# RWKV-6 layer with a ternary feed-forward on one Trainium2 core: work moved between VectorE and GpSimd, weight setup inside tile 0, another layout of the last feed-forward

## The chip, the cores and the metric

One core of a Trainium2 chip runs the whole kernel. TensorE multiplies matrices and writes to PSUM. VectorE and ScalarE read and write PSUM and SBUF. GpSimd works on SBUF alone. SyncE issues the DMAs. The engines run side by side and wait for each other on semaphores. The metric is the device time of one launch in microseconds; smaller is better.

## What is computed

Input x is [4, 2048, 512] in float32. The reference computes, in float32:

```
x = layernorm(x + attention(x))          # RWKV-6 time mixing, 16 heads of 32
x = layernorm(x + feed_forward(x))

attention:  xx = x_prev - x
            mix = tanh((x + xx * maa_x) @ maa_w1) @ maa_w2        # five mixes: w k v r g
            r, k, v, g = projections of x + xx * (maa_* + mix)
            decay = exp(-exp(time_decay + tanh(xw @ td_w1) @ td_w2))
            y_t = r_t (S + u k_t v_t);  S = decay_t S + k_t v_t   # scan over 2048 steps
            out = (groupnorm(y) * ln_g + ln_b) * silu(g) @ Wo
feed_forward: h = gelu(x @ ternary(W_fc)); h = layernorm(h) * ln_w + ln_b; h @ ternary(W_proj)
ternary(W) = sign(W) * min(round(|W| / (mean|W| + eps)), 1)
```

## The kernel before

The sequence is cut into 32 tiles of 64 steps (4 sequences, 256 columns a tile). `tile` on each engine does the attention of tile `it`; the pieces of the feed-forward of tile `it - 1` stand between its steps (`ffn.up`, `ffn.down`, ...), so that engines that wait for one have the other. `over_tiles` writes out tiles 0 (without a feed-forward) and 1, loops over 2 to 31 and ends with `feed_forward(31).alone()`. All orders are written by hand; every engine does its instructions strictly in that order.

Steps that the change and the prediction speak of, in the order of a tile:
- The five mixes. TensorE multiplies the low-rank mix (L385), VectorE makes `(mix + maa) * XX` (L1100), GpSimd adds x (L916; VectorE for the decay input, L1111). `XX` is x_prev - x of the tile; VectorE made it in `differences` (L1082) near the end of the tile before. `mixed_by_x` (L1088) makes x + xx * maa_x from XX and XT, and TensorE multiplies it by W1 (L364, L367).
- XT, the next tile's x, is loaded by SyncE (L306) once GpSimd's fourth L916 is done.
- The chunk's scores are built in levels of 1, 2, 4, 8, 16. VectorE writes the even rows of RB (L1192) and ScalarE the odd ones; TensorE multiplies (L464, L481 for each level); between levels VectorE scales R and K (`scale_right` L1166, `scale_left` L1177), copies queries (L1156) and gathers the products into A (L1206, L1226).
- A is copied by strips into AB; GpSimd copies the last strip (L940). TensorE forms the output of each pair of sequences from the state (L522) and from AB (L538).
- VectorE copies the output (L1239), weighs it with ln_g and the gate (L1266), adds to the state (L1247), multiplies G by ln_b (L1277), and scales by the group deviation (L1279 to L1293). TensorE multiplies by Wo (L616).
- Feed-forward: `up` is on TensorE (L641) the hidden layer, on ScalarE GELU (L852), the scaled fp16 high part HHI (L861) and the square (L863), on VectorE the low part HLO (L1351) and the running sums (L1340, L1343). `down` (L660) multiplies by W_proj. `moments`, `product`, `normed`, `stored` finish a pair; GpSimd takes their inverse roots (L909, `finish`, `normed`) and adds the bias (L971).

Setup: VectorE sums |W| of eight pieces (L1021), quantises them (L1054, L1057), centres Wv (L1068 to L1074); TensorE multiplies the scaled ln_w and ln_b by W_proj (`against_second`), from which WSUM and BSUM are kept; GpSimd zeroes buffers (L877, L879) and splits the mix weights into high and low parts (L888, L890).

## Time and profile before

| | us |
|---|---|
| median of 3 runs | 3076.63 |
| lowest and highest | 3074.3, 3081.04 |
| the profiled execution, as timed | 3077.73 |
| its span in the trace | 3075.9 |
| TensorE busy | 2895.1 (94%) |
| VectorE busy | 2488.6 (81%) |
| ScalarE busy | 1928.0 (63%) |
| GpSimd busy | 931.3 (30%) |

A busy share is a mean over the whole launch. What ends a stretch is read from the waits and from the timelines: a row there has the start in us, the duration, engine, line, operation, output and inputs with shapes, how many were merged, and in brackets how long the engine had been idle and what ended it. "issue" means that the profile names no releaser.

### The profile page before, as it was taken

The numbers are of one execution on the slowest core, as the hardware profiler recorded it, in microseconds if no ns is written. First come the engines' busy times: TensorE is split into PE (matmuls) and PEld (weight loads), VectorE is DVE, ScalarE is ACT, GpSimd is POOL, SyncE is SP. The second block draws the span as 40 slices with busy tenths as digits, with TensorE's granted clock in tenths as the row PEclk, the third lists the DMA queues.
The fourth block names the chain that finished last, engine by engine and source line by source line (L and its number), as shares of the span: only waits on it lengthen the run. The fifth ranks groups of instructions, "written<-read, shape, count | busy, mean of one in ns | idle before, by whom it ended". The sixth has DMA issues, their size and how long they took to land.

```text
span 3075.9 us, 101635 instructions
## 1 busy us (share of the span) xinstructions
PE 2895.1 (94%) x40249; PEld 2120.9 (69%) x40249; DVE 2488.6 (81%) x5435; ACT 1928.0 (63%) x4079; POOL 931.3 (30%) x790
## 2 busy tenths in 40 slices
PE   1889999999999999999999999999999999999997
PEld 0666677777677777677777676777677777767775
DVE  8467887788887788888788898788798788888777
ACT  0456676666676666676666576666567666667664
POOL 1223232333322333332233322233323233332232
PEclk9899999999999999999999999999999999999999
DMA  5000000000000000000000000000000000000000
GB/s 215 8 15 23 13 19 23 22 16 22 13 23 19 23 16 23 16 20 19 23 16 22 16 19 19 23 15 22 23 13 19 23 22 16 23 13 23 19 23 15
DMA packets 22822, 73.40 MB, mean 24 GB/s; under 512 B 3104, under 2 KB 3360, under 8 KB 20768
## 3 DMA queue, kind: packets, MB, share of 16 engines
q1 hardware_dynamic: 22432, 67.10, 6.4%
q8 instruction: 379, 6.21, 0.8%
q14 instruction: 11, 0.09, 0.0%
HBM read 50.31 MB, written 16.78 MB: 22 GB/s over the span
## 4 chain that ended last, share of the span: by engine, by line
PE 63%; DVE 23%; issue 9%; ACT 3%; DVEq 1%; DMA 1%; SPq 0%; ACTq 0%; POOLq 0%; POOL 0%
PE psP L404 18%; PE psF L641 11%; PE psP L442 7%; PE psP L616 6%; PE psF L660 4%; DVE HLO L1351 4%; DVE ARENA L1226 2%; PE psY L522 2%; PE psY L538 2%; DVE SUMS L1343 2%; DVE ARENA L1100 2%; DVE ARENA L1088 2%; DVE ARENA L1166 2%; DVE ARENA L1290 1%; PE psP L424 1%
## 5 line engine op out<-in xcount | busy, mean ns | idle before, releaser
L404 PE MATMUL psP<-ARENA,WALL 128*128 128x256 f32 x3072 | 694.2, 381 | 2.7 <-ACT ARENA L733 2.7
L690 ACT ACTIVATE ARENA<-ARENA 32x512 f32<-32x512 f32 (+3 forms) x930 | 524.2, 564 | 188.1 <-DVE ARENA L1166 92.5
L404 PEld LDWEIGHTS psP<-ARENA,WALL 128*128 128x128 f32 x3072 | 574.9, 190 | 79.3 <-issue 1.8
L1351 DVE SCALAR_TENSOR_TENSOR HLO<-GG,FWB,HHI 128x128 f16<-128x128 f32 x1024 | 347.5, 400 | 283.4 <-ACT HHI L861 278.4
L641 PE MATMUL psF<-XHI,WFC 128*128 128x128 f16 x4096 | 488.2, 220 | 2.2 <-DVE ST L1367 1.9
L641 PE MATMUL psF<-XLO,WFC 128*128 128x128 f16 x4096 | 486.6, 220 | 0.0
L902 POOL TENSOR_TENSOR MT<-ARENA 32x256 fp32r<-32x256 f32 x330 | 319.3, 968 | 445.3 <-ACT ARENA L690 416.7
L916 POOL TENSOR_TENSOR ARENA<-ARENA,XT 128x1024 f32<-128x1024 f32 x128 | 278.6, 2177 | 506.3 <-DVE ARENA L1100 506.3
L641 PEld LDWEIGHTS psF<-XHI,WFC 128*128 128x128 f16 x4096 | 397.9, 98 | 41.0 <-issue 32.9
L641 PEld LDWEIGHTS psF<-XLO,WFC 128*128 128x128 f16 x4096 | 402.0, 98 | 17.6 <-issue 10.3
L660 PE MATMUL psF<-WPJ,HHI 128*128 128x512 f16 x1024 | 390.6, 381 | 13.5 <-ACT GG L852 13.5
L660 PE MATMUL psF<-WPJ,HLO 128*128 128x512 f16 x1024 | 388.8, 380 | 0.0
L909 POOL TENSOR_TENSOR FV<-FV,CF 128x1 f32<-128x1 f32 x64 | 67.8, 1059 | 1009.3 <-DVE FV L1373 1009.3
L861 ACT ACTIVATE HHI<-GG,FWB 128x128 f16<-128x128 f32 x1024 | 327.4, 390 | 25.5
L852 ACT ACTIVATE GG<-psF 128x512 f32<-128x512 f32 x256 | 152.2, 595 | 250.1 <-PE psP L404 135.9
L616 PE MATMUL psP<-WALL,ARENA 128*128 128x512 f32 x512 | 235.2, 602 | 4.3 <-DVE ARENA L1293 2.4
L442 PE MATMUL psP<-WALL,ARENA 128*128 128x512 f32 x512 | 224.9, 592 | 0.0
L690 ACT ACTIVATE ARENA<-psP 128x256 f32<-128x256 f32 (+1 forms) x192 | 93.8, 528 | 171.3 <-PE psP L404 171.3
L660 PEld LDWEIGHTS psF<-WPJ,HHI 128*128 128x128 f16 x1024 | 99.9, 98 | 128.7 <-issue 19.0
L852 ACT ACT_TABLE_LOAD x62 | 79.5, 1283 | 158.1 <-PE psP L442 153.1
L1100 DVE SCALAR_TENSOR_TENSOR ARENA<-psX,PAR,XX 128x256 f32<-128x256 f32 x324 | 141.0, 477 | 39.4 <-PE psX L385 39.4
L481 PEld LDWEIGHTS psW<-ARENA 128*32 128x32 f32 x8192 | 123.2, 111 | 68.9 <-issue 68.9
(165 smaller groups left out, 5160.4 us busy)
## 6 DMA issues: line engine op xcount, KB each, us to landing
XT<-x_ch SPq DMA_DIRECT2D x33, 520.0 KB, 3.4
ARENA<-x_tok SPq DMA_DIRECT2D x32, 512.0 KB, 4.7
out<-OUT SPq DMA_DIRECT2D x64, 256.0 KB, 2.1
WALL<-w_all SPq DMA_DIRECT2D x5, 1024.0 KB, 15.5
ARENA<-wfc SPq DMA_DIRECT2D x4, 1024.0 KB, 8.2
ARENA<-wpj SPq DMA_DIRECT2D x3, 1024.0 KB, 14.8
GG<-wpj SPq DMA_DIRECT2D x1, 1024.0 KB, 18.9
OUT<-w2a SPq DMA_DIRECT2D x8, 64.0 KB, 14.0
```

The source lines that it names most:

```text
L404: mm = pe.matmul(psP[:, P.bank(f"{name}{g}"), COLS * c:COLS * (c + 1)], WALL[:, w, k, 128 * (2 * g + c):128 * (2 * g + c + 1)], cc(XF[slot ...
L442: mm = pe.matmul(psP[:, P.bank(f"v{p}"), :], cc(XF[1], k)[:, 128 * p:128 * (p + 1)], WALL[:, W_V, k, :], start=(k == 0), stop=(k == KC - 1))
L616: mm = pe.matmul(psP[:, P.bank(f"wo{p}"), :], cc(YSB, k)[:, 128 * p:128 * (p + 1)], WALL[:, W_O, k, :], start=(k == 0), stop=(k == KC - 1))
L641: mm = pe.matmul(psF[:, F.bank(name), 128 * m:128 * (m + 1)], WFC[:, k, 128 * (4 * g + m):128 * (4 * g + m + 1)], x[:, p, k, :], start=(k ...
L660: mm = pe.matmul(psF[:, F.bank(f"pj_{p}"), :], h[:, m, :], WPJ[:, m, :], start=(m == 0 and h is HHI), stop=(m == MH - 1 and h is HLO))
L690: return act.activation(o, i, ACT.Copy)
L852: act.activation(GG[:, u % 2, 0, :], psF[:, F.bank(f"fc{g}_{p}"), :], ACT.Gelu).then_inc(f_act, 1)
L861: e = act.activation(HHI[:, k, :], GG[:, u % 2, 0, 128 * m:128 * (m + 1)], ACT.Copy, scale=FWB[:, 0, k:k + 1])
L902: pool.tensor_tensor(MT[f][rows(1 + 2 * (n % 2)), :], whole, high, ALU.subtract).then_inc(mt_low, 1)
L916: pool.tensor_tensor(v, v, xcur, ALU.add).then_inc(xf_ready, 1)
L1100: e = dve.scalar_tensor_tensor(out=cc(XF[(f + 1) % 2], k), in0=M_BANKS[M.bank(f"{name}{g}")][:, COLS * c:COLS * (c + 1)], scalar=PAR[:, k, ...
L1351: e = dve.scalar_tensor_tensor(out=HLO[:, k, :], in0=GG[:, u % 2, 0, 128 * m:128 * (m + 1)], scalar=FWB[:, 0, k:k + 1], in1=HHI[:, k, :], ...
```

## The change

It has four parts.
1. The mix weights (now one broadcast load a rank, on the semaphore `mixing_in`) and XT are loaded ahead of the other weights, and W_proj last. The constants' small steps come first on VectorE. Only W_fc is quantised ahead of tile 0. W_proj is summed, quantised and multiplied (`against_second`, in quarters) between the steps of tile 0, and WSUM and BSUM are kept at its end.
2. GpSimd computes XX (`differences`) after the bias, and multiplies G by ln_b in one operation; VectorE does neither any more.
3. GpSimd copies its AB strip ahead of the root of `finish`; VectorE does `up(1, 0)` ahead of `normed`.
4. The last feed-forward (`alone`) writes the hidden layer of pair 1 to four banks of the attention, between the `down` products of pair 0, and the product and sums of pair 1 to two others.

```diff
-        RAW = ([ARENA1[:, 2048 * k:2048 * (k + 1)] for k in range(4)] + [ARENA2[:, 2048 * k:2048 * (k + 1)] for k in range(3)]
-               + [GG[:, :, :, :].rearrange("p i s n -> p (i s n)")])
+        RAW = ([ARENA1[:, 6144:8192]] + [ARENA2[:, 2048 * k:2048 * (k + 1)] for k in range(3)]
+               + [ARENA1[:, 2048 * k:2048 * (k + 1)] for k in range(3)] + [GG[:, :, :, :].rearrange("p i s n -> p (i s n)")])
...
+            sp.dma_start(XT[:, :, :], x_ch[0]).then_inc(xt_in, 16)
+            sp.dma_start(W1[:, :, :], w1).then_inc(mixing_in, 16)
+            for f in range(5):
+                rank = w2a[rows(f), :] if f < 4 else w2b
+                sp.dma_start(W2RAW[f // 2][:, f % 2, :], rank.unsqueeze(0).broadcast_to([4, MIXR, C])).then_inc(mixing_in, 16)
+            sp.dma_start(WALL[:, W_V, :, :], w_all[:, W_V, :, :]).then_inc(values_in, 16)
+            for dst, src in ((TD1[:, :, :], td1), (TD2[0:DECR, :], td2), (TD2[DECR:2 * DECR, :], td2),
+                             (WALL[:, W_K, :, :], w_all[:, W_K, :, :])):
+                sp.dma_start(dst, src).then_inc(weights_in, 16)
+            for w in (W_R, W_G, W_O):
+                sp.dma_start(WALL[:, w, :, :], w_all[:, w, :, :]).then_inc(weights_in, 16)
...
+            def against_second(v, part):
+
+                if part == 0:
+                    pe.wait_ge(su_dve, 3)
+                    pe.wait_ge(quantised, 8)
+                for m in range(MH // 4 * part, MH // 4 * (part + 1)):
+                    for n, h in enumerate((VHI, VLO)):
+                        mm = pe.matmul(psF[:, v, :], h[:, v, m:m + 1].broadcast_to([128, 128]), WPJ[:, m, :],
+                                       start=(m == 0 and n == 0), stop=(m == MH - 1 and n == 1))
+                if part == 3:
+                    mm.then_inc(su_pe, 1)
+
+            pe.wait_ge(mixing_in, 16 * NMIXING)
...
+                if first:
+                    second_magnitude()
                 mix(it - 1, 3, "mr", wait_free)
+                if first:
+                    pe.wait_ge(su_dve, 5)
...
+                    if first:
+                        against_second(0, i)
...
-                    for p in range(PAIRS):
-                        for g in range(4):
-                            up(p, g)
-                        for part in range(4):
-                            down(j, p, part)
-                        stats(j, p)
+                    for g in range(4):
+                        up(0, g)
+                    pe.wait_ge(p_dve, P.read(tiles - 1, "wo1"))
+                    pe.wait_ge(w_dve, W.read(j, "xt1"))
+                    for g in range(4):
+                        hidden(LAST_UP[g], 1, g).then_inc(last_up, 1)
+                        down(j, 0, g)
+                    stats(j, 0)
+                    pe.wait_ge(m_dve, M.read(tiles, "mk1"))
+                    for g in range(4):
+                        pe.wait_ge(hlo_ready, 8 * j + 4 + g + 1)
+                        mm = projected(LAST_PRODUCT[:, :], g)
+                    mm.then_inc(last_product, 1)
+                    pe.wait_ge(sums_folded, 2 * (PAIRS * j + 1) + 2)
+                    summed(LAST_STATS).then_inc(last_stats, 1)
...
-            pool.wait_ge(quantised, 4)
-            pool.memset(ARENA1[:, 0:6144], 0.0).then_inc(su_pool, 1)
-            pool.wait_ge(quantised, 8)
-            pool.memset(ARENA2[:, 0:512], 0.0).then_inc(su_pool, 1)
...
+            def differences(it):
+                pool.wait_ge(xt_in, 16 * (it + 1))
+                pool.tensor_tensor(XX[:, :, :], xprev, xcur, ALU.subtract).then_inc(xx_ready, 1)
...
+                if first:
+                    pool.wait_ge(quantised, 7)
+                    pool.memset(ARENA1[:, 0:6144], 0.0).then_inc(su_pool, 1)
                 if ffn:
                     ffn.bias()
-                    ffn.finish()
+                differences(it + 1)
...
+                if ffn:
+                    ffn.finish()
...
+                pool.wait_ge(y_weighed, it + 1)
+                pool.tensor_tensor(G.rearrange("p (c t) -> p c t", c=KC), G.rearrange("p (c t) -> p c t", c=KC),
+                                   PAR[:, :, LN_B:LN_B + 1].broadcast_to([128, KC, COLS]), ALU.mult).then_inc(y_affine, 1)
 
                 pool.wait_ge(s_decayed, it + 1)
+                pool.wait_ge(y_affine, it + 1)
...
+            magnitudes(0, range(4), 6)
+            thresholds(0, psP[:, 0, 0:1], 6)
+            for k in range(4):
+                quantise(k, 8 + k)
+            dve.wait_ge(quantised, 4)
...
+            centred_values()
+            magnitudes(1, (0, 1), None)
...
+                if first:
+                    magnitudes(1, (2, 3), 16)
...
+                if first:
+                    thresholds(1, psF[:, 0, 0:1], 16)
+                    quantise(4, 18)
+                    quantise(5, 19)
...
+                if first:
+                    quantise(6, 20)
+                    quantise(7, 21)
...
-                dve.wait_ge(m_dve, M.read(it, "mg1"))
-                differences(it + 1)
...
                 if ffn:
+                    ffn.up(1, 0)
                     ffn.normed()
-                if ffn:
-                    ffn.up(1, 0)
...
-                dve.wait_ge(y_weighed, it + 1)
-                for k in range(KC):
-                    dve.tensor_scalar(cc(G, k), cc(G, k), PAR[:, k, LN_B:LN_B + 1], None, ALU.mult).then_inc(y_affine, 1)
...
+                    for g in range(4):
+                        up(0, g)
+                    fold(j, 0)
+                    for g in range(4):
+                        up(1, g)
+                    moments(j, 0)
+                    fold(j, 1)
+                    product(j, 0)
+                    normed(j, 0)
+                    stored(j, 0)
+                    moments(j, 1, last=True)
+                    product(j, 1, last=True)
+                    normed(j, 1)
+                    stored(j, 1)
```

GpSimd's order in a tile with a feed-forward (tile 1, which is written out; the loop's body has the same order). OUT is the bias step, CF the AB strip, FV and OSD the two roots, TOT the state's decay, MT the mix's low parts. Before:

```order
L916 TENSOR_TENSOR ARENA<-ARENA,XT 128x1024
L971 TENSOR_TENSOR OUT<-X,BSUM 128x512 x2
L909 TENSOR_TENSOR FV<-FV,CF 128x1
L940 TENSOR_TENSOR ARENA<-ARENA,CF 32x16x32
L948 TENSOR_TENSOR ARENA<-ARENA,TOT 128x512
L909 TENSOR_TENSOR OSD<-OSD,CF 128x1
L902 TENSOR_TENSOR MT<-ARENA 32x256 x10
```

And now:

```order
L964 TENSOR_TENSOR ARENA<-ARENA,XT 128x1024
L1029 TENSOR_TENSOR OUT<-X,BSUM 128x512 x2
L957 TENSOR_TENSOR XX<-XT 128x1024
L992 TENSOR_TENSOR ARENA<-ARENA,CF 32x16x32
L953 TENSOR_TENSOR FV<-FV,CF 128x1
L1002 TENSOR_TENSOR ARENA<-ARENA,TOT 128x512
L953 TENSOR_TENSOR OSD<-OSD,CF 128x1
L1006 TENSOR_TENSOR ARENA<-ARENA,PAR 128x1024
L943 TENSOR_TENSOR MT<-ARENA 32x256 x10
```

XX (L957) and the ln_b product (L1006) are new, and the AB strip (L992) stands ahead of the first root.

VectorE in tile 0, from the mix for v to the rows of RB (L1100, now L1169, is a mix; TOT are the decay totals; WPJ is the quantised W_proj). Before, with the five smaller TOT steps between the second row and the third left out:

```order
L1100 SCALAR_TENSOR_TENSOR ARENA<-psY,PAR,XX 128x256 x2
L1138 TENSOR_TENSOR TOT<-ARENA 128x512
...
L1138 TENSOR_TENSOR TOT<-TOT 128x16
L1100 SCALAR_TENSOR_TENSOR ARENA<-psX,PAR,XX 128x256 x2
L1100 SCALAR_TENSOR_TENSOR ARENA<-psY,PAR,XX 128x256 x2
L1192 TENSOR_TENSOR ARENA<-ARENA,PAR 32x4x64 x8
```

And now the stretch that ends with the same step, from the mix for r:

```order
L1169 SCALAR_TENSOR_TENSOR ARENA<-psY,PAR,XX 128x256 x2
L1109 TENSOR_SCALAR SC<-psF 128x1
...
L1121 TENSOR_SCALAR HHI<-ARENA,SC 128x2048
L1123 SCALAR_TENSOR_TENSOR WPJ<-ARENA,SC,HHI 128x2048
...
L1169 SCALAR_TENSOR_TENSOR ARENA<-psY,PAR,XX 128x256 x2
L1121 TENSOR_SCALAR HHI<-ARENA,SC 128x2048
L1123 SCALAR_TENSOR_TENSOR WPJ<-ARENA,SC,HHI 128x2048
L1121 TENSOR_SCALAR HHI<-GG,SC 128x2048
L1123 SCALAR_TENSOR_TENSOR WPJ<-GG,SC,HHI 128x2048
L1271 TENSOR_TENSOR ARENA<-ARENA,PAR 32x4x64 x8
```

Two pieces are quantised behind the mix for r and two behind the mix for g, all ahead of the rows of RB.

VectorE in tile 1, from the copy of pair 1's output to the group deviation. Before:

```order
L1082 TENSOR_TENSOR XX<-XT 128x1024
...
L1239 COPY ARENA<-psY 128x4x128
L1391 BN_STATS FBN<-OUT 128x6
...
L1351 SCALAR_TENSOR_TENSOR HLO<-GG,FWB,HHI 128x128 x4
L1266 SCALAR_TENSOR_TENSOR ARENA<-ARENA,PAR 128x256 x4
...
L1088 SCALAR_TENSOR_TENSOR ARENA<-XX,PAR,XT 128x256 x4
...
L1277 TENSOR_SCALAR ARENA<-ARENA,PAR 128x256 x4
L1279 RECIPROCAL RS<-psP 128x32
```

And now:

```order
L1318 COPY ARENA<-psY 128x4x128
L1426 SCALAR_TENSOR_TENSOR HLO<-GG,FWB,HHI 128x128 x4
L1473 BN_STATS FBN<-OUT 128x6
...
L1342 SCALAR_TENSOR_TENSOR ARENA<-ARENA,PAR 128x256 x4
...
L1157 SCALAR_TENSOR_TENSOR ARENA<-XX,PAR,XT 128x256 x4
...
L1415 TENSOR_TENSOR SUMS<-GG 128x1024
L1352 RECIPROCAL RS<-psP 128x32
```

The XX step and the ln_b step are gone, and HLO (L1426) stands ahead of the bn steps.

## Rows read from the trace of the kernel before

**Rows 1.** Windows by stage: length, busy us of each engine, clock, DMA, GB/s.
```profile
93.75:182.00 88.25, 73.13 (x938) 53.54 (x938) 49.35 (x101) 38.31 (x75) 20.52 (x18) 0.81 0.04 13
275.00:3026.00 2751.00, 2674.00 (x37610) 1964.31 (x37609) 2264.29 (x5048) 1802.94 (x3809) 854.72 (x721) 1.00 0.06 19
```
**Rows 2.** Waits, 275 to 3026 us: waiter, releaser: us in total, times, longest.
```profile
PE psY L538 <- issue: 41.8, 30, 1.5
PE psW L481 <- DVE ARENA L1177: 11.2, 30, 0.5
```
**Rows 3.** Timelines of VectorE, GpSimd and TensorE around the last AB strip.
```profile
2901.29 1.23 DVE L1082 TENSOR_TENSOR XX<-XT 128x1024 f32<-128x1024 f32 x1
2901.32 1.60 POOL L909 TENSOR_TENSOR FV<-FV,CF 128x1 f32<-128x1 f32 x1 [31.54 <-DVE FV L1373]
2903.16 1.27 POOL L940 TENSOR_TENSOR ARENA<-ARENA,CF 32x512 f32<-32x512 f32 x1 [0.24 <-POOL FV L909]
2904.53 1.08 PE L538 MATMUL psY<-ARENA,V 128*32 128x128 f32 x32 [1.46 <-issue]
```
**Rows 4.** Timelines of VectorE and TensorE, same tile, around L1088.
```profile
2908.36 1.67 DVE L1266 SCALAR_TENSOR_TENSOR ARENA<-ARENA,PAR 128x256 f32<-128x256 f32 x4
2910.74 0.42 DVE L1247 TENSOR_TENSOR ARENA<-ARENA,psX 128x256 f32<-128x256 f32 x1 [0.71 <-PE psX L566]
2911.41 1.67 DVE L1088 SCALAR_TENSOR_TENSOR ARENA<-XX,PAR,XT 128x256 f32<-128x256 f32 x4
...
2913.29 1.91 PE L364 MATMUL psX<-ARENA,W 128*128 128x256 f32 x8
```
**Rows 5.** Timelines of VectorE and GpSimd where both work on SBUF.
```profile
2921.55 0.71 DVE L1293 TENSOR_TENSOR ARENA<-ARENA 128x512 f32<-128x512 f32 x1
2922.19 0.81 DVE L1351 SCALAR_TENSOR_TENSOR HLO<-GG,FWB,HHI 128x128 f16<-128x128 f32 x1
...
2921.80 1.05 POOL L902 TENSOR_TENSOR MT<-ARENA 32x256 fp32r<-32x256 f32 x1
```
**Rows 6.** Timelines of VectorE, GpSimd and SyncE around the load of XT.
```profile
2865.14 2.18 POOL L916 TENSOR_TENSOR ARENA<-ARENA,XT 128x1024 f32<-128x1024 f32 x1 [5.49 <-DVE ARENA L1100]
2867.49 0.35 SPq L306 DMA_DIRECT2D XT<-x_ch  x1
2870.64 1.21 DVE L1340 TENSOR_TENSOR SUMS<-GG 128x1024 f32<-128x1024 f32 x1
2871.77 3.44 DVE L1192 TENSOR_TENSOR ARENA<-ARENA,PAR 32x256 f32<-32x256 f32 x8
2876.88 0.43 DVE L1156 COPY ARENA<-ARENA 32x512 f32<-32x512 f32 x1 [0.27 <-PE psW L464]
```
**Rows 7.** The page's part 6, DMA issues: count, KB each, us to landing.
```profile
XT<-x_ch SPq DMA_DIRECT2D x33, 520.0 KB, 3.4
```
**Rows 8.** Timelines of VectorE and TensorE in the levels.
```profile
2888.36 0.68 DVE L1177 TENSOR_TENSOR ARENA<-ARENA,TOT 128x512 f32<-128x512 f32 x1
...
2889.28 0.54 PE L481 MATMUL psW<-ARENA 128*32 128x64 f32 x23 [0.46 <-DVE ARENA L1177]
```
**Rows 9.** Timelines of the setup.
```profile
42.69 1.29 DVE L1054 TENSOR_SCALAR HHI<-ARENA,SC 128x2048 f16<-128x2048 f32 x1
44.01 2.35 DVE L1057 SCALAR_TENSOR_TENSOR WFC<-ARENA,SC,HHI 128x2048 f16<-128x2048 f32 x1
46.42 5.22 POOL L877 MEMSET ARENA<- 128x6144 f32 x1 [45.97 <-DVE WFC L1057]
73.62 2.40 POOL L890 TENSOR_TENSOR W2S<-OUT,W2S 64x1024 fp32r<-64x1024 f32 x1
80.11 3.75 PE L364 MATMUL psX<-ARENA,W 128*128 128x256 f32 x8 [3.61 <-DVE ARENA L1088]
93.75 0.87 DVE L1100 SCALAR_TENSOR_TENSOR ARENA<-psX,PAR,XX 128x256 f32<-128x256 f32 x2
```
**Rows 10.** Timeline of VectorE in tile 0.
```profile
127.33 3.45 DVE L1192 TENSOR_TENSOR ARENA<-ARENA,PAR 32x256 f32<-32x256 f32 x8 [6.05 <-ACT ARENA L690]
```
**Rows 11.** Timeline of ScalarE in the last feed-forward, pair 1.
```profile
3053.56 0.60 ACT L852 ACTIVATE GG<-psF 128x512 f32<-128x512 f32 x1 [7.18 <-PE psF L641]
```

More of the change, by code:

```diff
@@ L648, in stats @@
                     F.wait_free(pe, j, f"st_{p}", first)
-                    for i in range(2):
-                        mm = pe.matmul(psF[:, F.bank(f"st_{p}"), i:i + 1], GR[:, i, :], ONES[:, 0:1], start=True, stop=True)
-                    mm.then_inc(f_full, 1)
+                    summed(psF[:, F.bank(f"st_{p}"), :]).then_inc(f_full, 1)
                 def down(j, p, part):
@@ L1316, in tile @@
                     ffn.stored()
+                if first:
+                    sums_of_second()
             def feed_forward(j, before):
```

231 lines of the change are left out of this document (119 added, 112 removed).

## The prediction

> **What bounds the kernel now.** I read the windows by stage first. From 275 us to 3026 us (tiles 2 to 31) TensorE is busy for 2674.0 of 2751.0 us at the full clock [rows 1], so a tile of 91.7 us leaves it 2.6 us idle. Next come the waits of that stretch: of that idle time 41.8 us in 30 tiles stand before one matmul group, L538, 1.5 us a time, and 11.2 us before L481, behind VectorE's L1177 [rows 2]. The rest is crumbs. The timelines then show that VectorE is no spare engine here. L481 starts 0.24 us after L1177 ends [rows 8], and the four levels before it and after it are one chain VectorE, ScalarE, TensorE with no slack. So two engines bound a tile in turn, and any microsecond taken from VectorE between its L1192 and the last L481 is a microsecond of the tile. The start is a chain of DMA, VectorE and one long TensorE product up to 93.75 us [rows 9], then tile 0 at a mean granted clock of 0.81 [rows 1].
>
> **The loop, part one: the wait before L538.** L538 (pair 1) needs the AB strip that GpSimd copies at L940. GpSimd first takes a root, L909, and that one is stretched to 1.60 us because VectorE's L1082 holds it up; L940 then ends at 2904.43 and L538 starts at 2904.53, after 1.46 us of idle time [rows 3]. After the change L1082 isn't there and the copy stands ahead of the root. The pair-0 output that it waits for ends at 2899.05, so the copy ends at about 2900.4, 2.7 us before TensorE comes (2903.07). Its other inputs were ready by 2901.6. The whole 1.46 us goes from this place.
>
> **Part two: LN_B on GpSimd.** VectorE loses the four L1277 (1.13 us), but it stood waiting for ScalarE behind them (L1351 starts as soon as ScalarE's HHI is there), so this buys nothing. GpSimd gains one operation of 128x1024, about 2.18 us like L916 [rows 6]. It may start when L1266 is done. With L538 1.46 us earlier, L1266 ends near 2909.0 (L1351 now stands ahead of the bn steps), so the operation runs 2909.1 to 2911.3. VectorE's two L1247 come at 2909.3, its L1088 at 2909.95 instead of 2911.41 [rows 4]. L1088 reads XX and XT, both in SBUF.
>
> What happens to such an operation can be read in [rows 5]: GpSimd's L902 arrives while VectorE's L1293 (two SBUF inputs) runs; it takes 1.05 us where it takes 0.72 us alone, and VectorE's next, L1351, takes 0.81 where alone it takes 0.35: it ends 0.15 us after L902. So they exclude each other, a waiting GpSimd goes before VectorE's next instruction, and each lets go some 0.14 us before its end. L1088 in the setup shows it from the other side: beside GpSimd's 2.40 us subtract [rows 9] the four together took 7.29 us, and 1.67 us in a tile [rows 4].
>
> So L1088 waits for the LN_B operation and ends its first quarter 0.28 us after it, at 2911.5 instead of 2910.4: 1.1 us lost. TensorE's L364 waits for L1088 (2913.08, start 2913.29) [rows 4]. Of the 1.46 us, 1.46 - 1.11 = **0.35 us** is left per tile.
>
> **Part three: XX on GpSimd.** The differences move from VectorE, where they lay beside TensorE's work, to GpSimd, 2.18 us [rows 6]. They need the next XT, which SyncE asks for at 2867.49 [rows 6] and which lands 3.4 us later [rows 7], at 2870.9. Just then VectorE is in L1340 (two SBUF inputs, to 2871.85), and back to back behind it stand the eight L1192, the first members of the critical chain [rows 6]. By [rows 5] GpSimd gets in at 2871.7, ends at 2873.9, and the first L1192 ends at 2874.1 instead of 2872.18: 1.93 us lost. Of this 0.23 us is taken up by the wait before L1156 (0.27 us [rows 6]); the rest arrives at L1177, and L481 follows L1177 [rows 8]. Cost: **1.7 us** per tile. Bounds: 0 if L1192 does not collide after all, 2.18 if nothing is absorbed.
>
> The Trainium skill ("SBUF — State Buffer", section Who interferes with whom) says the same more strictly: a VectorE instruction with two SBUF inputs and a GpSimd instruction that reads SBUF share one port pair, and the second waits until the first has finished. By that rule without the 0.14 us at each end, XX would cost 2.0 us instead of 1.7, and the sum would be 10 us higher.
>
> Loop: 31 tiles with a feed-forward (1 to 31) x (1.70 - 0.35) = **+42 us**. Who is late next is VectorE in the levels, and TensorE's idle time moves from L538 to L464, L481 and L364.
>
> **The start.** Now: eight pieces are summed, eight quantised, TensorE's first real product L364 starts at 80.11, and VectorE takes the first mixed input at 93.75, after TensorE has multiplied the second half of the sums [rows 9]. After: the first weight's four sums end at 17.6 as now (each 2.29 us, bound by landing), thresholds by 19.2. Four pieces at 1.29 + 2.35 us [rows 9] are 14.6 us. GpSimd's six W2S operations (2.40 [rows 9], 2.40, 1.26, 1.12, 1.12, 0.69: 9.0 us) now start when their weights land, near 21.5, and exclude both kinds of VectorE instruction, so the two add up: 43.0. Then XX 1.2 and four L1088 1.7: L364 starts at 45.9, **34 us** earlier. From L364 to the mixed input no product of 7.6 us stands between; VectorE is next bound by itself, with 4.8 us of centring and two sums of 2.3 us: 55.3 instead of 93.75, **38.4 us** earlier.
>
> Tile 0 pays most of this back. VectorE waited some 22 us between 93.75 and L1192 at 127.33 [rows 10]. The two later sums (4.9 us) fit into one such wait. Then come in its queue: thresholds 0.7, two pieces 7.4, two GpSimd operations that shut them out 3.2, the mix for g, two pieces 7.4, with GpSimd's L916 in between 2.2, the 5.22 us memset [rows 9] that the last piece waits for (as L1054 did in the setup), and XX 2.2, all before L1192. I get the end of the L1192 at 108.3 instead of 130.8 - 38.4 = 92.4: 15.9 us back. The eight quarters of the sums' products (1.9 us each) lie between level steps and outputs where TensorE waits; some 2 us of them show. WSUM and BSUM (1.4 us) lie at the tile's end, half hidden. TensorE idles 13 us before L464, so the clock may be at the lower level when it resumes, as it was for part of tile 0 before (0.81) [rows 1]: 0 to 3 us. Start: 38.4 - 15.9 - 2.2 - 0.7 - 1.5 = **18 us** gained, between 10 and 24.
>
> **The end.** ScalarE waited 7.18 us for the second pair's hidden layer [rows 11]; with banks of the attention it doesn't. But VectorE finishes pair 0 now only after pair 1's last sum, 6 us of small steps that stood in that wait before. Pair 1's moments start at 3065.8 instead of 3068.6: **3 us** gained, between 0 and 5.
>
> **Sum.** The profiled execution took 3077.73 us, its span 3075.9; it lies 1.1 us above the median of 3076.63. 3077.7 + 42 - 18 - 3 = 3098.7; less a median's distance, **3098 us**.
>
> **Rivals.**
> One: XX collides with nothing on the path. For it: no row shows an L1192 beside a GpSimd operation, and a landing before 2870.6 would move XX ahead of L1340. Against: L1192 has the two SBUF inputs of L1293 and L1088, and even an earlier XX delays L1340, which is in the same chain. Time: 3098 - 31 x 1.7 = 3045 us. Chance 0.12.
> Two: no collision counts, neither XX nor LN_B. Then 1.46 us x 31 = 45 us is gained: 3077.7 - 45 - 21 = 3012 us. Against it speak the rows of the two engines [rows 5]. Chance 0.05.
> Three: collisions cost about half, since GpSimd's arrival shifts with the tile or VectorE finds slack I don't see: net 0 to 0.7 us a tile, 3057 to 3078 us. Chance 0.13.
> Four, slower still: the start gives nothing, because TensorE comes back from its 13 us wait at the lower clock and tile 0's quantising pieces each collide; the point from which this decides is L464 later than 115 us. With it 3098 + 12 = 3110, and up to 3125 if XX also costs its full 2.18. Chance 0.12.
> That the change doesn't do what it says: DMA landing of the mixing weights after 35 us instead of 21.5 would leave L364 near 55; that is inside the range.
> My forecast: 0.58, its own range 3085 to 3112.
>
> **Numbers.** Leaving out the two fast rivals (0.17) gives the range 3060 to 3122. About 0.2% (6 us) is what a measurement of this kernel can tell from none. Faster by more than that: rivals one and two and half of three, 0.24; within: 0.08; slower: 0.68.
>
> **What would show it.** Right: the L538 wait gone; the line of XX on GpSimd at 2.2 us or more, and the first L1192 of each tile at some 2.3 us instead of 0.42; the first L1088 at 1.6 us instead of 0.48; TensorE waiting about 2 us a tile before L464 and L481 for VectorE; a tile of 93 us instead of 91.7; L364 first at 46 us; L1192 of tile 0 ending near 108 us. Wrong: L1192 at 0.42 us each with XX beside it, or a tile under 91.5 us.

## The result, and the profile after

The changed kernel takes 3082.86 us (median of 16 runs, 3079.39 to 3088.01), the one before 3077.53 us (16 runs, 3072.02 to 3081.04). The ratio is 1.002 with a 95% interval of 1.0012 to 1.0028: slower by 0.2%, and the interval leaves out 1. Forecast were 3098 us, slower by 0.7%. The sign is right and the time lies in the range, but the loss is a quarter of what was forecast. The profiled execution of the changed kernel has a span of 3079.4 us, against 3075.9.

Three numbers split the difference. The first is the start of the first matmul of L476 (L464 before), with which the levels of a tile begin on TensorE; its rows name the first of tile 0 and the last of tile 31 (columns: count; shortest, median and longest in ns; start of the first and of the last in us; shapes, with how many of a sample have them).

TensorE's line L464 of the kernel before:

```profile
L464 PE MATMUL psW<-ARENA x2048: 270/273/297, 130.1 to 2969.0; 128*32 128x128 f32 x187
```

The same matmuls, L476, of the changed kernel:

```profile
L476 PE MATMUL psW<-ARENA x2048: 269/273/421, 104.7 to 2975.3; 128*32 128x128 f32 x187
```

- Up to the levels of tile 0: 104.7 against 130.1, **25.4 us gained**.
- The 31 tiles from there: 2975.3 - 104.7 = 2870.6 against 2838.9, **31.7 us lost**. From one tile's first L1271 (L1192 before) to the next, tiles 3 to 29 take 92.68 us on average against 91.62.
- The end: 3079.4 - 2975.3 = 104.1 against 106.9, **2.8 us gained**.

The sum, -25.4 + 31.7 - 2.8, is the 3.5 us between the spans. So a large gain in the start and a large loss in the loop nearly cancel. The waits of the loop show the loss. TensorE's waits of the changed kernel, 275 to 3026 us (waiter, releaser: us in total, times, longest):

```profile
PE psW L493 <- DVE ARENA L1254: 44.4, 60, 1.0
PE psF L660 <- issue: 17.5, 20, 1.5
PE psF L673 <- ACT GG L900: 7.8, 30, 0.3
PE psX L372 <- DVE ARENA L1157: 6.4, 10, 0.7
```

The wait before the last strip's product is gone, as forecast: 41.8 us stood there in [rows 2]. In its place stand 44.4 us before the levels' L493 (11.2 us before, as L481), 6.4 us before L372, and something that no step of the prediction had: 17.5 us inside the group L660, with "issue" as its cause, which is time in which the engine waited for nothing that the profile shows.

**The collision of XX with the levels.** GpSimd and VectorE of the changed kernel in tile 30, and the lines of all tiles (columns as above):

```profile
2876.02 2.97 POOL L957 TENSOR_TENSOR XX<-XT 128x1024 f32<-128x1024 f32 x1 [1.18 <-DMA XT<-x_ch]
...
2875.69 1.21 DVE L1415 TENSOR_TENSOR SUMS<-GG 128x1024 f32<-128x1024 f32 x1
2876.83 3.31 DVE L1271 TENSOR_TENSOR ARENA<-ARENA,PAR 32x256 f32<-32x256 f32 x4
...
L957 POOL TENSOR_TENSOR XX<-XT x32: 2740/2960/3242, 97.8 to 2968.6; 128x1024 f32<-128x1024 f32 x32
...
L1271 DVE TENSOR_TENSOR ARENA<-ARENA,PAR x256: 406/418/2022, 102.7 to 2974.0; 32x256 f32<-32x256 f32 x128
```

XX is asked for during L1415, as forecast, ends at 2878.99, and one L1271 takes 2.02 us instead of 0.42. But it is the second one, not the first: the first (2876.83 to 2877.23) went ahead of XX, which the trace has as begun at 2876.02. It is so in all 31 tiles with a feed-forward. The second product ends 0.28 us behind XX. The eight L1271 end 1.6 us late instead of 1.93, and the last level group of TensorE starts 1.38 us later after the first L1271 than before (21.73 against 20.35 us, mean of 27 tiles).

**The hole in L660.** TensorE of the changed kernel, tile 30, behind the second L552:

```profile
2910.96 0.22 PE L660 MATMUL psF<-XHI,WFC 128*128 128x128 f16 x1
2911.02 0.22 PE L660 MATMUL psF<-XLO,WFC 128*128 128x128 f16 x1
2911.92 0.23 PE L660 MATMUL psF<-XHI,WFC 128*128 128x128 f16 x1 [0.69 <-issue]
2911.99 0.22 PE L660 MATMUL psF<-XLO,WFC 128*128 128x128 f16 x1
```

These matmuls belong to one group that waits for nothing between its first and its last, and they come every 0.056 us. Behind the eighth there is a hole of 0.69 us. It stands in 19 of the 27 tiles from 3 to 29, each time behind the eighth matmul, and is 0.67 to 1.51 us long. The DMA view of the stretch just ahead of it (2909.5 to 2911.0 us) has one packet of instructions among the data:

```profile
q1 hardware_dynamic: 24, 0.04, 8.4%
q8 instruction: 1, 0.02, 4.0%
```

That packet (16 KB) moved from 2909.74 to 2910.70. In all 19 tiles with a hole the last packet of instructions before it landed 1.24 to 1.46 us ahead of the hole's end, however long the hole was. In the 8 tiles without one this packet had started 30.9 to 31.5 us after the first L1271 of the tile instead of 32.7 to 33.5. This looks like TensorE waiting for its own program: the loop's body has 2,600 recorded instructions of TensorE (1,254 matmuls, as many weight loads and 92 others), and 12 packets of 16 KB come in each tile. In the kernel before, the 1.46 us wait before L538 stood just ahead of this place and covered it. Runs e6 and e11 test this.

**The start.** VectorE, GpSimd and TensorE of the changed kernel:

```profile
35.02 4.57 DVE L1157 SCALAR_TENSOR_TENSOR ARENA<-XX,PAR,XT 128x256 f32<-128x256 f32 x4
...
52.02 2.29 DVE L1098 TENSOR_REDUCE SUMS<-ARENA 128x32 f32<-128x2048 f32 x1 [6.28 <-DMA ARENA<-wpj]
54.49 2.29 DVE L1098 TENSOR_REDUCE SUMS<-ARENA 128x32 f32<-128x2048 f32 x1 [0.19 <-DMA ARENA<-wpj]
56.69 0.87 DVE L1169 SCALAR_TENSOR_TENSOR ARENA<-psX,PAR,XX 128x256 f32<-128x256 f32 x2
...
35.80 1.04 POOL L929 CAST W2S<-OUT 128x1024 fp32r<-128x1024 f32 x1 [35.35 <-DMA V<-w2b]
...
39.74 3.75 PE L372 MATMUL psX<-ARENA,W 128*128 128x256 f32 x8 [21.29 <-DVE ARENA L1157]
```

The last of the W2S weights landed at 35.7, not at 21.5 (35.35 in GpSimd's row is how long it had been idle), so GpSimd did not disturb the quantising, and L372 (L364 before) started at 39.7 instead of the forecast 45.9. This lead was lost again: VectorE stood in its queue before the second weight's sums, whose weights landed at 52.0 and 54.5, though the product for its mix was ready at 50.4. The mix came at 56.7 (forecast 55.3, before 93.75).

**The clock in tile 0.** The same stretch of both kernels, from the first matmul of the levels over the length of tile 0 (columns as in [rows 1]), first before, then changed:

```profile
130.05:216.20 86.15, 72.78 (x1018) 54.39 (x1018) 53.71 (x112) 45.77 (x92) 23.30 (x20) 0.86 0.04 14
104.70:190.50 85.80, 81.04 (x1078) 56.28 (x1079) 53.17 (x106) 43.56 (x87) 28.09 (x22) 0.95 0.05 14
```

The mean granted clock is 0.95 instead of 0.86: TensorE stood at the lower of its two levels (1.2 GHz) for 7.9 us of the stretch instead of 23.9. It also has more to do there, since the products of the second weight now lie in this tile, and it is busy for 81.0 us instead of 72.8.

### The profile page after: what moved, and what is told of

Same layout as the page of the kernel before. It is cut to its first block, busy times and chain, and to the rows that moved or that the text cites. A ratio compares the mean times of both kernels' runs of the same rounds, so it can differ in the third digit from the quotient of the medians.

```text
span 3079.4 us, 101531 instructions
## 1 busy us (share of the span) xinstructions
PE 2898.8 (94%) x40249; PEld 2114.4 (69%) x40249; DVE 2499.3 (81%) x5277; ACT 1929.1 (63%) x4079; POOL 1061.7 (34%) x854
## 4 chain that ended last, share of the span: by engine, by line
PE 52%; DVE 30%; issue 11%; ACT 4%; DVEq 1%; SPq 1%; DMA 1%; ACTq 0%; POOL 0%; POOLq 0%
PE psP L412 11%; PE psF L660 10%; PE psP L454 7%; PE psP L638 6%; DVE HLO L1426 5%; DVE ARENA L1271 5%; PE psF L673 3%; DVE ARENA L1305 3%; ACT HHI L909 3%; PE psY L536 2%; DVE ARENA L1169 2%; PE psY L552 2%; DVE SUMS L1415 2%; DVE SUMS L1418 2%; DVE ARENA L1243 2%
## 5 line engine op out<-in xcount | busy, mean ns | idle before, releaser
L1426 DVE SCALAR_TENSOR_TENSOR HLO<-GG,FWB,HHI 128x128 f16<-128x128 f32 x1024 | 347.6, 400 | 327.1 <-ACT HHI L909 322.2
L660 PE MATMUL psF<-XHI,WFC 128*128 128x128 f16 x4032 | 482.7, 220 | 19.2 <-issue 17.5
L660 PE MATMUL psF<-XLO,WFC 128*128 128x128 f16 x4032 | 480.9, 219 | 0.0
L660 PEld LDWEIGHTS psF<-XHI,WFC 128*128 128x128 f16 x4032 | 390.9, 98 | 61.2 <-issue 53.7
L660 PEld LDWEIGHTS psF<-XLO,WFC 128*128 128x128 f16 x4032 | 395.5, 98 | 17.6 <-issue 10.3
L673 PE MATMUL psF<-WPJ,HHI 128*128 128x512 f16 x1008 | 383.5, 380 | 10.6 <-ACT GG L900 10.6
L673 PE MATMUL psF<-WPJ,HLO 128*128 128x512 f16 x1008 | 381.9, 379 | 0.0
L909 ACT ACTIVATE HHI<-GG,FWB 128x128 f16<-128x128 f32 x1024 | 327.2, 390 | 25.4
L992 POOL TENSOR_TENSOR ARENA<-ARENA,CF 32x512 f32<-32x512 f32 x32 | 40.6, 1268 | 853.0 <-PE psY L552 853.0
L493 PEld LDWEIGHTS psW<-ARENA 128*32 128x32 f32 x8192 | 122.0, 110 | 99.3 <-issue 99.3
L493 PE MATMUL psW<-ARENA 128*32 128x64 f32 x8192 | 140.9, 220 | 45.5 <-DVE ARENA L1254 44.4
```

The costliest lines, as they stand in the source:

```text
L493: mm = pe.matmul(psW[BLK * (q % 4):BLK * (q % 4 + 1), W.bank(name), o:o + 64], cc(KM, c)[:, BLK * q:BLK * (q + 1)], RB[RB_SEQ[name]][:, c, ...
L660: mm = pe.matmul(bank[:, 128 * m:128 * (m + 1)], WFC[:, k, 128 * (4 * g + m):128 * (4 * g + m + 1)], x[:, p, k, :], start=(k == 0 and part ...
L673: mm = pe.matmul(bank, h[:, m, :], WPJ[:, m, :], start=(m == 0 and h is HHI), stop=(m == MH - 1 and h is HLO))
L909: e = act.activation(HHI[:, k, :], GG[:, u % 2, 0, 128 * m:128 * (m + 1)], ACT.Copy, scale=FWB[:, 0, k:k + 1])
L1426: e = dve.scalar_tensor_tensor(out=HLO[:, k, :], in0=GG[:, u % 2, 0, 128 * m:128 * (m + 1)], scalar=FWB[:, 0, k:k + 1], in1=HHI[:, k, :], ...
```

## The experiments

Each was run beside the kernel before on the same chip (3074.9 to 3076.8 us there). Tile lengths are means of tiles 3 to 29, from the start of the level products L1271 to the next, in one profiled execution each. e6, e11 and e12 were timed once, the other e-runs 4 times and e2 10 times. Two parts of one edit are shown with "..." between them; a semaphore count that follows from an edit is left out.

| run | what it is | us | tile, us |
| --- | --- | --- | --- |
| before | | 3077.5 | 91.62 |
| changed | | 3082.9 | 92.68 |
| e1 | changed, XX on VectorE | 3035.8 | 91.10 |
| e2 | changed, LN_B on VectorE | 3078.7 | 92.56 |
| e3 | changed, both on VectorE | 3025.1 | 90.86 |
| e4 | before, strip ahead of the root | 3052.6 | 90.83 |
| e5 | changed, XX later on GpSimd | 3038.0 | 91.24 |
| e6 | changed, 64 waits more (timed once) | 3071.4 | 92.38 |
| e7 | e3, XX behind the product | 3027.1 | 90.86 |
| e8 | e7, sums behind the mix | 3017.5 | 90.89 |
| e9 | e8, 64 waits more | 3005.9 | 90.24 |
| e10 | e8, 128 waits more | 3016.5 | 90.71 |
| e11 | changed, 8 waits more (timed once) | 3084.4 | 92.76 |
| e12 | e2, 64 waits more (timed once) | 3049.4 | 91.64 |

### e1: XX back on VectorE

The first piece is GpSimd's, the second VectorE's:

```diff
                     ffn.bias()
-                differences(it + 1)
                 pool.wait_ge(k1_odd, it + 1)
-                pool.wait_ge(xx_ready, it + 2)
...
                     ffn.stats()
+                dve.wait_ge(m_dve, M.read(it, "mg1"))
+                differences(it + 1)
                 if ffn:
                     ffn.finish()
```

> The changed kernel with the differences XX back on VectorE, at their old place behind the fold of pair 0. Measured so far: the changed kernel takes 3082.86 us, the one before 3077.53; a tile takes 92.66 us against 91.63. Theory (GpSimd's XX shuts out the eight products L1271 that head the levels, and that costs 1.36 us a tile at the levels' last TensorE groups): 3082.9 - 31 x 1.36 = 3041 us, the second L1271 of a tile back at 0.42 us from 2.02. If VectorE's 1.22 us for XX, now behind a strip that no longer waits for it, shows on the path: up to 3041 + 31 x 1.2 = 3078. Rival (it is the longer work of GpSimd as such, or the supply of TensorE's instructions, that made the tile longer): 3075 to 3083, no change.

Measured: 3035.79 us (ratio 0.987, 0.9854 to 0.9887), 47 us less than the changed kernel, and the level products are never held up:

```profile
L1265 DVE TENSOR_TENSOR ARENA<-ARENA,PAR x256: 406/417/455, 100.9 to 2926.5; 32x256 f32<-32x256 f32 x128
```

The one move of XX to GpSimd made the change lose; without it the change gains 1.3%. It is worth 1.58 us a tile, 0.2 more than the 1.38 at the levels. The rest lies in TensorE's gaps further on, which are 0.59 us a tile behind the last strip here and 0.81 (hole and wait before L372 together) in the changed kernel.

### e2: the product by LN_B back on VectorE

Again GpSimd's piece first:

```diff
-                pool.wait_ge(y_weighed, it + 1)
-                pool.tensor_tensor(G.rearrange("p (c t) -> p c t", c=KC), G.rearrange("p (c t) -> p c t", c=KC),
-                                   PAR[:, :, LN_B:LN_B + 1].broadcast_to([128, KC, COLS]), ALU.mult).then_inc(y_affine, 1)
...
                     ffn.up(1, 1)
+                dve.wait_ge(y_weighed, it + 1)
+                for k in range(KC):
+                    dve.tensor_scalar(cc(G, k), cc(G, k), PAR[:, k, LN_B:LN_B + 1], None, ALU.mult).then_inc(y_affine, 1)
```

> The changed kernel with the product by LN_B back on VectorE as four small products; XX stays on GpSimd. Theory A (the product on GpSimd holds up L1157 by 1.1 us in every tile, as forecast): 3083 - 31 x 1.03 = 3051 us. Theory B (it holds it up only in the tiles in which TensorE has no hole inside its group L660 after the last strip; in 19 of 27 tiles of the trace that hole, 0.67 to 1.51 us long and each time behind the eighth matmul pair, has already delayed L1157's inputs, so that the product is out of the way): the 0.66 us of some 8 tiles goes, 3083 - 6 = 3077, and the hole is there in nearly every tile.

Measured: 3078.72 us (ratio 1.0009, 1.0 to 1.0019), 4 us less than the changed kernel, a tile 0.12 us shorter: theory B. No wait before L372 is left, but the hole is longer (20.0 us instead of 17.5 from 275 to 3026 us):

```profile
PE psF L660 <- issue: 20.0, 23, 1.5
```

Hole and collision cover each other, so neither can be priced by taking one of them away.

### e3: both back on VectorE

> The changed kernel with both XX and the product by LN_B back on VectorE: new start, new end and the strip ahead of the root are left. Theory: start -25.0, end -2.5, the wait before L552's second group -1.43 a tile, and of this the hole in L660 takes back about 0.9: 3077.5 - 27.5 - 31 x 0.53 = 3034 us. Without the hole 3006. Rival (the two operations on VectorE cost on the path what they did not show before): 3050 to 3078.

Measured: 3025.07 us (ratio 0.9835, 0.9818 to 0.9851). The edit is that of e1 and e2 together. The theory's 3034 us was 9 us too many: the hole took 0.1 us a tile, not 0.9. Still the tile of 90.86 us is only 0.77 less than before, not 1.46. Waits of e3, 275 to 2950 us:

```profile
PE psF L660 <- DVE OUT L1461: 12.7, 30, 0.5
PE psF L673 <- ACT GG L900: 7.5, 29, 0.3
PE psF L660 <- issue: 3.4, 8, 0.6
```

Behind the strip TensorE needs the PSUM bank that VectorE's L1461 (the product of pair 0) reads last, and on VectorE XX stands ahead of it. This is the wait that was next behind L538's, and the prediction has no term for it.

### e4: the strip ahead of the root, alone

On GpSimd, in the kernel before:

```diff
                 if ffn:
                     ffn.bias()
-                    ffn.finish()
...
                 pool.wait_ge(ab_rest, it + 1)
+                if ffn:
+                    ffn.finish()
```

> The kernel before with one edit alone: GpSimd copies the last AB strip ahead of the root instead of behind it. If the whole 1.46 us wait before L538 is gained in 30 tiles: 3077.5 - 44 = 3033 us. If TensorE's instructions arrive too late once it doesn't wait (the hole in the group behind it, some 0.9 us a tile): 3077.5 - 31 x 0.55 = 3060 us, with a hole behind the eighth pair of L641's group. Rival (the strip was late for another reason): 3077.

Measured: 3052.62 us (ratio 0.9918, 0.9902 to 0.9935): 24 us, or 0.79 a tile, half of what the wait was worth. It lies between the two cases, since two things share the rest (waits, 275 to 2950 us):

```profile
PE psF L641 <- DVE OUT L1386: 12.2, 29, 0.6
...
PE psF L641 <- issue: 3.9, 11, 0.6
```

So the hole comes up in the kernel before too, once the strip's wait is gone.

### e5: XX on GpSimd, at another place

On GpSimd, behind the strip and the root:

```diff
                     ffn.bias()
-                differences(it + 1)
                 pool.wait_ge(k1_odd, it + 1)
-                pool.wait_ge(xx_ready, it + 2)
...
                 if ffn:
                     ffn.finish()
+                differences(it + 1)
+                pool.wait_ge(xx_ready, it + 2)
                 pool.wait_ge(tot_ready, NPL * it + 6)
```

> The changed kernel with XX still on GpSimd, but behind the AB strip and the root of pair 0 instead of ahead of the strip: the same operation on the same engine at another place, where VectorE's neighbours are products that read PSUM. The product by LN_B stays on GpSimd. Theory (the cost of XX is the collision with L1271, not GpSimd's 1.90 us as such): the second L1271 back from 2.02 to 0.42 us and a tile of 91.1 us or less; about 3036 us as with XX on VectorE (run e1), and up to 12 us less, since there TensorE's group behind the last strip also waited 0.4 us a tile for VectorE's product behind XX. Rival (any GpSimd operation of this length costs its time on this path): 3075 to 3083.

Measured: 3037.99 us (ratio 0.9879, 0.9863 to 0.9896). The same operation on the same engine costs 45 us less at this place, and it takes 1.89 us instead of 2.96. The two long VectorE operations beside it read PSUM (the row of L957 in all tiles, then one tile):

```profile
L957 POOL TENSOR_TENSOR XX<-XT x32: 1892/1893/1953, 127.0 to 2956.5; 128x1024 f32<-128x1024 f32 x32
...
1130.55 1.89 POOL L957 TENSOR_TENSOR XX<-XT 128x1024 f32<-128x1024 f32 x1
...
1129.91 0.76 DVE L1462 SCALAR_TENSOR_TENSOR psF<-WSUM,ST,psF 128x512 f32<-128x512 f32 x1
1130.62 0.21 DVE L1464 TENSOR_SCALAR FSC<-FV,SC 128x1 f32<-128x1 f32 x1
1130.87 0.75 DVE L1467 SCALAR_TENSOR_TENSOR OUT<-psF,FSC,OUT 128x512 f32<-128x512 f32 x1
```

The further 12 us did not come. The hole (15.7 us in 19 tiles) and L372's wait (6.4 us in 10; both 275 to 2950 us) fill the place.

### e6: 64 waits more in TensorE's setup

```diff
+            for _ in range(64):
+                pe.wait_ge(su_dve, 4)
             pe.wait_ge(mixing_in, 16 * NMIXING)
```

> The changed kernel with 64 waits that are already satisfied put into TensorE's queue in the setup: no data and no order changes, but every later instruction of TensorE stands 64 places further back. Theory (the hole behind the eighth matmul pair of group L660 is a wait for the next block of TensorE's instructions; in the trace it ends 1.24 to 1.46 us after one 16 KB instruction packet has landed, and is missing in the tiles where that packet landed earlier): the hole moves 64 instructions ahead, into the group L552 or the one before it, and is no longer behind the eighth pair. Rival (the hole is a wait for data or for a PSUM bank): it stays behind the eighth pair of that L660 group. The time moves little in both, 3075 to 3090.

Measured, in one run: 3071.35 us, a tile of 92.38 us. The hole behind the eighth matmul is gone in all 27 tiles. Now every tile waits before L372 (line L374 here) for VectorE (275 to 2950 us):

```profile
PE psX L374 <- DVE ARENA L1159: 16.1, 29, 0.7
PE psF L675 <- ACT GG L902: 7.5, 29, 0.3
PE psY L554 <- issue: 0.3, 1, 0.3
```

A wait for data would not care about 64 satisfied waits in the setup, so the rival falls. The hole did show elsewhere, ahead of its old place as expected, but it is so short that the waits hardly list it (the 0.3 us of L554, line L552 without the edit). In 14 of the 27 tiles the 25th matmul of the second L554 group starts 0.37 us after the 24th, where its neighbours follow every 0.03 us. This place lies 32 recorded instructions ahead of the old one, and 32 is what the 64 waits are in the trace: TensorE has 48 recorded semaphore instructions up to the levels of tile 0 instead of 16.

And the collision of the LN_B product with the mix by x, forecast in every tile, is there as soon as the hole doesn't cover it. VectorE and GpSimd of e6, one tile:

```profile
1983.60 2.07 DVE L1159 SCALAR_TENSOR_TENSOR ARENA<-XX,PAR,XT 128x256 f32<-128x256 f32 x3
...
1982.69 1.90 POOL L1008 TENSOR_TENSOR ARENA<-ARENA,PAR 128x1024 f32<-128x1024 f32 x1 [0.86 <-DVE ARENA L1344]
```

The first quarter takes 1.27 us here instead of 0.48 (1.11 to 1.31, mean 1.20, in the 27 tiles) and ends 0.28 us behind GpSimd's product, as forecast. The product itself takes 1.90 us, not 2.18.

### e7: XX on VectorE behind the product

On VectorE, from e3:

```diff
-                dve.wait_ge(m_dve, M.read(it, "mg1"))
-                differences(it + 1)
                 if ffn:
                     ffn.finish()
+                dve.wait_ge(m_dve, M.read(it, "mg1"))
+                differences(it + 1)
                 outputs(1)
```

> Run e3 (both operations on VectorE, 3025 us) with XX behind the product of pair 0 on VectorE instead of ahead of it. In e3 TensorE's group behind the last strip waits 0.42 us a tile for that product, which frees its PSUM bank, and which waits for XX (1.23 us) and for a root that XX stretches to 1.60 us. Theory: this wait goes, 0.4 us x 31 = 13 us: 3012 us. Rival (the hole in the supply of TensorE's instructions comes up to the same point and takes its place, as it did when the strip's wait went): 3020 to 3025, with a hole of 0.7 us or more in most tiles.

Measured: 3027.09 us (ratio 0.984, 0.9824 to 0.9857), no gain over e3. The 12.7 us wait for the product is gone, and the hole came up in its place, as the rival said (275 to 2950 us, 3.4 us in e3):

```profile
PE psF L660 <- issue: 16.4, 20, 1.2
```

### e8: the sums behind the first mix

On VectorE, from e7:

```diff
-            magnitudes(1, (0, 1), None)
             decay_input(-1)
             dve.wait_ge(tm_ready, M.read(-1, "w1b"))
             mix(0, 1, "mk", None)
+            magnitudes(1, (0, 1), None)
```

> Run e7 with one more edit in the setup: VectorE takes the two sums of the second weight after the first mixed input instead of ahead of it. In the trace of the changed kernel these sums wait for the weight's landing (52.0 and 54.5 us), while the product that the mix needs is ready at 50.4; the mix came at 56.7. Theory: the mix comes 6 us earlier, and tile 0, where VectorE is the bound between 64 and 106 us, gives back the sums' 4.6 us and more: 0 to 3 us less than e7. Rival (the mix is on the path up to tile 0's levels): 6 us less than e7.

Measured: 3017.54 us (ratio 0.9814, 0.9792 to 0.9836), 9.5 us less than e7 (runs of 3013.8 to 3025.5 against 3022.9 to 3028.3). The mix starts at 50.5 and the levels of tile 0 at 97.4, 4.9 us earlier than in e7. So the first mix is on the path up to tile 0's levels, as the rival had it. Behind them tile 0 takes 84.8 us instead of 87.8, with TensorE at its lower clock level for 6.2 us instead of 12.0; the two profiled executions differ by 6.7 us in all.

### e9 and e10: e8 with 64 and with 128 waits more

> Run e8 (3017.5 us) with the 64 satisfied waits of run e6 in TensorE's queue. In e6 the hole in group L660 didn't move to another group, it was gone in all 27 tiles. Theory (supply of instructions, which has slack at the new place): the hole of e8 (18 of 27 tiles, 0.57 us a tile) goes, a tile takes 90.3 us instead of 90.89, in all 3017.5 - 31 x 0.57 = 3000 us. Rival (e6's hole was covered by the collision of the product by LN_B, which e8 doesn't have): the hole stays or another comes, 3013 to 3020 us.

> Run e8 with 128 satisfied waits instead of 64. Theory (supply of instructions by blocks, so that the hole depends on which instruction of the loop begins a block): another time than e8 and e9, anywhere between 2998 and 3025 us, with its hole, if it has one, at another instruction than e8's. Rival (what helps is that TensorE starts later, or a fixed cost): the same as e9 within 2 us.

Measured: e9 3005.92 us (ratio 0.9778, 0.9762 to 0.9795), e10 3016.46 us (0.9817, 0.9801 to 0.9834). In e9 the hole in L660 is gone and a tile takes 90.24 us. The edit is worth 11.6 us though it computes nothing. What is left of the hole, from 275 to 2950 us, and TensorE in a tile that has it:

```profile
PE psY L554 <- issue: 1.1, 3, 0.4
...
2288.66 0.86 PE L554 MATMUL psY<-ARENA,V 128*32 128x128 f32 x24
2289.89 0.42 PE L554 MATMUL psY<-ARENA,V 128*32 128x128 f32 x8 [0.37 <-issue]
```

With 128 waits a part is lost again. TensorE of e10 in one tile:

```profile
2662.81 0.42 PE L554 MATMUL psY<-ARENA,V 128*32 128x128 f32 x8
2663.63 0.64 PE L554 MATMUL psY<-ARENA,V 128*32 128x128 f32 x15 [0.40 <-issue]
```

In 18 of the 27 tiles of e10 the ninth matmul of the second L554 starts 0.38 to 0.67 us after the eighth, and in 13 tiles there is a shorter hole inside the first L554. So the places follow the shift: behind the eighth matmul of L660 without waits, 32 recorded instructions earlier (behind the 24th of L554) with 64 waits, 64 earlier (behind the eighth of L554) with 128. It isn't the later start that helps, it is where the program's parts begin. e9 is the fastest of all, 2.2% below the kernel before.

Counted back from the branch that ends the loop's body, in TensorE's recorded instructions, the holes of one kernel lie 256 apart: at 616 and 360 (e7), at 620 and 364 (e11), at 936, 680 and 424 (e10). So the program comes in parts of 256 instructions, and one part would be one packet of 16 KB. The number of packets agrees: TensorE's 2,600 and the other engines' 574 recorded instructions of a tile are 12.4 such parts, and 12 packets come.

### e11: 8 waits more

> The changed kernel with 8 satisfied waits in TensorE's setup. Theory (the hole stands at the first instruction of a block): in the tiles that have it, it moves from behind the eighth matmul of group L660 to 8 instructions earlier, which is behind the fourth, since each matmul stands with a weight load of its own. A tile stays at 92.6 us. Rival (a wait for data or a bank): behind the eighth, as before.

Measured, in one run: 3084.37 us. The hole moved, in all 23 tiles that have it, from behind the eighth to behind the sixth matmul of the group:

```profile
2913.42 0.22 PE L662 MATMUL psF<-XHI,WFC 128*128 128x128 f16 x1
2913.48 0.22 PE L662 MATMUL psF<-XLO,WFC 128*128 128x128 f16 x1
2914.75 0.23 PE L662 MATMUL psF<-XHI,WFC 128*128 128x128 f16 x1 [1.06 <-issue]
```

Expected was the fourth, with 8 instructions for 8 waits. But the trace has only 4 recorded semaphore instructions more up to the levels of tile 0 (20 instead of 16), and two matmuls with their two weight loads are 4 instructions. Nothing but the place in the instruction stream was changed by 4, and the hole moved by 4.

### e12: the LN_B product on VectorE, without the hole

> Run e6 (changed kernel with 64 satisfied waits, no hole, a tile of 92.38 us) with the product by LN_B back on VectorE. In e6 the first L1157 of each tile takes 1.27 us instead of 0.48 and ends 0.28 us behind GpSimd's product. Theory (the collision is real and was only covered by the hole in e2): a tile of 92.38 - 0.79 = 91.6 us, so 0.8 us less than e6, where without the 64 waits the same edit gave 0.12 (92.68 to 92.56). Rival (it costs nothing on the path): 92.3 us.

Measured, in one run: 3049.4 us, and a tile of 91.64 us: 0.73 less than e6, as against 0.12 for the same edit with the hole in place. So the product on GpSimd does cost 0.7 us a tile.

## Why the prediction was right in its sign and wrong in its size

**The step that failed.** The mechanisms of the loop were right: the strip's wait goes, and each of GpSimd's two new operations holds up a VectorE instruction on the path. Two terms of the sum were mis-sized, both towards a slower kernel. The loop was put at +42 us and measured +31.7, because the term of XX, 31 x 1.70, had GpSimd's operation at 2.18 us where it takes 1.89. The start was put at -18 us and measured -25.4, because what tile 0 was to pay back was booked too high: 15.9 us ahead of its levels and 4.4 behind. The forecast loss of 21 us was a small difference between large terms, so these misses of 10 and 7 us left only a quarter of it.

**The strip (right, and the step behind it missing).** The 1.46 us before L538 went as forecast: the last strip's product starts 32.71 us after the first L1271 of its tile against 32.78, though the levels ahead of it are 1.38 us late, so 1.4 us are gained. What is late next was looked for on VectorE and found only in part: with XX and LN_B left where they were (e4), the gain is 0.79. The bank that L1461 frees, 0.4 us a tile (e3, e4), and the program's supply, 0.1 to 0.5 (e3, e4, e7), take the rest. In the trace of before neither could be seen: the wait of [rows 3] covered both.

**LN_B (mechanism right, size near, hidden by something else).** The forecast 1.11 us a tile is 0.73 where nothing hides it (e12 against e6). The operation was priced by GpSimd's 128x1024 add of 2.18 us [rows 6] and takes 1.90; that is 0.28 of the difference. In the changed kernel the collision shows in 8 tiles of 27 only: there the first L1157 takes 1.12 to 1.30 us instead of 0.48. In the other 19 the hole had put off L372's inputs until GpSimd was done. So strip and LN_B together, forecast at 0.35 gained, came to about 0.3 (1.38 lost at the levels, 1.06 in the whole tile). This near hit is luck: the gain of 1.46 shrank to 0.79 (e4) and the loss of 1.11 to 0.12 (e2), or to 0.73 with the hole away, and a hole of 0.62 us a tile, for which the sum has no term, lay over part of it.

**XX (mechanism right, mis-sized).** Forecast 1.70 us a tile, measured 1.38 at the levels. XX takes 1.89 us (e5), not 2.18, and that 0.29 is nearly the whole miss in size. The order was wrong too, without changing the size: XX did not go in before VectorE's next instruction, as [rows 5] had shown it, but one later. The absorbed 0.23 us was right: 1.6 us late at the products, 1.38 at the last level group. Over 31 tiles these 0.3 us are 10 of the 17 us by which the sum (20.9 us) missed what the two profiled executions show (3.5). The Trainium skill ("SBUF — State Buffer", section Who interferes with whom) has GpSimd operations that read SBUF and VectorE operations with two SBUF inputs exclude each other; the traces agree (2.02 instead of 0.42 us here, 1.27 instead of 0.48 in e6), and e5 agrees from the other side, since beside VectorE's long instructions that read PSUM the same XX took 1.89 us. In the order they differ from it: the page has the one that was issued first go first, and here XX, recorded as begun 0.8 us on average before the first L1271, was passed by it.

**The start (gain under-estimated).** Forecast: 22.5 us gained at the levels of tile 0 and 4.4 of them given back behind it, so 18. Measured: 25.4, and nothing visible given back: tile 0 takes 85.8 us from its first L1271 to the next, against 86.2 before.

Ahead of the levels the miss is 2.9 us. The mix came 1.4 us later than forecast, but VectorE took 49.5 us from there to the end of the L1271 instead of 53.0, and TensorE began 0.8 us sooner behind the first of them than before. The four collisions that were booked in it (3.2, 2.2, 5.2 and 2.2 us) took 10.7 us instead of 12.8; what made the rest was not separated.

Behind the levels the 4.4 us were eight products, WSUM and BSUM, and 1.5 us for a clock at the lower level. The clock went the other way, with 16 us less at the lower level in this stretch than before. Nine traces with the same setup (the changed kernel, e1 to e3, e5 to e7, e11, e12) tell what this is worth: tile 0 takes 84.8 to 86.0 us in the six with 6.1 to 8.2 us at the lower level, and 87.8 to 88.2 us in the three with 12.0 to 12.6, some 0.5 us more for each of them. By that the clock gave back about 8 us, an estimate, and the added work cost about as much, more than the 2.9 us booked for it. No run takes the two apart.

**The end.** Forecast 3 us, measured 2.8.

**The rivals.** XX colliding with nothing (3045 us) and no collision at all (3012 us) are refuted for the changed kernel. Their times are near to what e1 and e5 (3036 and 3038, XX's collision away) and e3 (3025, both away) reach. The third, a loop that loses 0 to 0.7 us a tile, gives up to 3078 us; the tile lost 1.06. The fourth is refuted by its own sign: the levels of tile 0 started at 104.7, not later than 115.

**What stays open.** Why the instruction packet is late in 19 tiles and early in 8 was not found; nor how far ahead TensorE's program is loaded, so that the place of the holes can be worked out but their length only measured. Start times also differ between runs of like kernels by some us, and with them TensorE's clock there: over all timed launches of the kernel before that have it on record, those at a mean granted clock of 0.994 or 0.995 took 3070.8 to 3071.8 us, and those at 0.991 took 3076.1 to 3079.5. So differences under 5 us between e-runs are not read here but for the tile lengths.

## What to carry to other kernels

Before work is moved from VectorE to an idle GpSimd, look at which VectorE instructions stand at the moment when its input arrives: the same subtract cost 45 us more beside products of two SBUF inputs at the head of a critical chain than beside instructions that read PSUM (e5). When a wait on the busiest engine is removed, ask what else it covered (a PSUM bank, a neighbour's collision, the loading of the program), since half of its worth can go there (24 of 45 us were left in e4). And read a gap inside one matmul group as a question to the instruction stream: shift the program by a few instructions and see whether the gap moves.
